# Cross-attention and FP4 feed-forward: gate and up in three chunks of 512, 512 and 384 columns in place of four of 352

## What is computed

```python
def fp4_linear(x, w):
    return einsum('bsk,nk->bsn', fp4_quant_dequant(x), fp4_quant_dequant(w))
def ffn(x, w_gate, w_up, w_down):          # w_gate, w_up: 1408 x 512, w_down: 512 x 1408
    gate, y = fp4_linear(x, w_gate), fp4_linear(x, w_up)
    h = silu(gate) * y
    return fp4_linear(h, w_down)
x = x + xattn(layernorm(x), ctx, ctx, mask, Wq, bq, Wk, bk, Wv, bv, Wo, bo)
x = x + ffn(layernorm(x), w_gate, w_up, w_down)
```

## Time and profile before

| | us |
|---|---|
| median of 3 executions (lowest, highest) | 2033.88 (2031.81, 2034.55) |
| the profiled execution | 2031.19 |
| its span, first to last instruction | 2029.3 |
| TensorE busy | 1898.9 (94%) |
| VectorE busy | 1770.0 (87%) |
| ScalarE busy | 1266.9 (62%) |
| GpSimd busy | 448.8 (22%) |

### The profile page before, as it was taken

How to read it: one execution, slowest core, us unless ns; L and a number is a source line. 1 busy time by engine, 2 the same in 40 slices (tenths; PEclk the granted TensorE clock), 3 DMA queues, 4 the chain that set the end, 5 groups by cost and what they waited for, 6 DMA issues and landing times.

```text
span 2029.3 us, 48669 instructions
## 1 busy us (share of the span) xinstructions
PE 1898.9 (94%) x17724; PEld 1192.0 (59%) x17792; DVE 1770.0 (87%) x2676; ACT 1266.9 (62%) x2613; POOL 448.8 (22%) x526
## 2 busy tenths in 40 slices
PE   6446899999999999999999999999999999999987
PEld 4334566656665666656665666666665666666643
DVE  7898889888899889888899889888899889888874
ACT  4575766676666666676666666676667666676421
POOL 5554221122112221122112211222112211222100
PEclk8667999999999999999999999999999999999998
DMA  5344566565766566566666566556765566556623
GB/s 170 105 114 95 109 144 144 127 132 132 156 133 132 130 145 139 129 133 134 149 138 132 130 147 138 127 134 136 154 131 132 130 149 137 126 134 133 128 56 84
DMA packets 716996, 265.34 MB, mean 131 GB/s; under 512 B 667930, under 2 KB 669878, under 8 KB 716958
## 3 DMA queue, kind: packets, MB, share of 16 engines
q1 hardware_dynamic: 715374, 264.85, 58.9%
q10 hardware_dynamic: 1584, 0.01, 0.1%
HBM read 66.34 MB, written 34.86 MB: 50 GB/s over the span
## 4 chain that ended last, share of the span: by engine, by line
PE 86%; DVE 6%; DMA 3%; issue 2%; POOL 1%; SPq 1%; ACT 1%; DVEq 0%; POOLq 0%; another core or an unknown queue 0%; ACTq 0%
PE psum L724 44%; PE psum L660 38%; PE psum L737 2%; PE psum L766 2%; DMA t_room<-halves 1%; DVE h_room L1278 1%; SPq L345 1%; PE psum L755 1%; POOL h_room L560 1%; DVE w_sc L1258 1%; POOL h_room L564 1%; DMA ph_room<-h_room 1%; DVE wguT L1246 1%; DVE h_room L1320 0%; DMA q_room<-in_L_xattn_Wk_dram 0%
## 5 line engine op out<-in xcount | busy, mean ns | idle before, releaser
L724 PE MATMUL psum<-wguT,t_room 128*128 128x352 bf16 x6144 | 943.1, 314 | 15.5 <-DVE h_room L1426 9.0
L724 PEld LDWEIGHTS psum<-wguT,t_room 128*128 128x128 bf16 x6144 | 597.4, 98 | 346.4 <-DVE h_room L1426 10.4
L660 PE MATMUL psum<-wdT,ph_room 128*128 128x512 bf16 x2108 | 469.8, 381 | 11.2 <-DMA ph_room<-h_room 10.9
L581 POOL TENSOR_TENSOR ln_var_eps<-ln_mean_var,eps 128x1 f32<-128x1 f32 x128 | 103.8, 811 | 1185.7 <-DVE ln_mean_var L1394 998.6
L660 PEld LDWEIGHTS psum<-wdT,ph_room 128*128 128x128 bf16 x2112 | 207.6, 98 | 263.3 <-issue 17.4
L982 ACT ACTIVATE silu_g<-psum 128x352 f32<-128x352 f32 x256 | 117.4, 459 | 380.2 <-PE psum L724 377.1
L988 ACT ACTIVATE probs<-psum,neg_max 128x77 f32<-128x77 f32 x1024 | 244.3, 350 | 3.7 <-DVE neg_max L1432 3.0
L1426 DVE TENSOR_TENSOR h_room<-silu_g,psum 128x352 f32<-128x352 f32 x256 | 132.2, 517 | 81.3 <-ACT silu_g L982 81.1
L1019 ACT ACTIVATE t_room<-psum,bq_col 128x128 bf16<-128x128 f32 x256 | 72.9, 367 | 185.7 <-PE psum L660 185.7
L660 PE MATMUL psum<-t_room,wqT 128*128 128x128 bf16 x3072 | 187.6, 222 | 0.8 <-DMA t_room<-halves 0.8
L660 PEld LDWEIGHTS psum<-t_room,wqT 128*128 128x128 bf16 x3072 | 177.7, 100 | 1.5 <-DMA t_room<-halves 1.1
(11 more groups left out here) (105 smaller groups left out, 2498.8 us busy)
## 6 DMA issues: line engine op xcount, KB each, us to landing
io_room<-in_x_dram SPq DMA_DIRECT2D x128, 256.0 KB, 2.8
x_scratch<-x_new SPq DMA_DIRECT2D x64, 256.0 KB, 2.0
x_cur<-x_scratch SPq DMA_DIRECT2D x64, 256.0 KB, 3.3
out_dram<-io_room SPq DMA_DIRECT2D x64, 256.0 KB, 2.4
t_room<-halves SPq DMA_TRANSPOSE x192, 3.2
raw<-in_L_ffn_w_down_dram SPq DMA_DIRECT2D x4, 704.0 KB, 4.3
raw<-in_L_ffn_w_gate_dram SPq DMA_DIRECT2D x11, 256.0 KB, 2.7
raw<-in_L_ffn_w_up_dram SPq DMA_DIRECT2D x11, 256.0 KB, 2.9
```

The costliest lines, as they stand in the source:

```text
L581: own.did(pool.tensor_tensor(var_eps, mean_var[:, 1:2], eps[:], ALU.add))
L660: ins = pe.matmul(dst, left(i), right(j), start=first and n == 0, stop=last and n == len(PRODUCTS) - 1)
L724: ins = pe.matmul(ps[:, 0:CW], left[:, i, kc, :], wguT[:, which, j, kc, cols], start=(kc == 0 and i == j), stop=(kc == KC - 1 and i == LO))
```

## The change

Gate and up are computed in chunks of 512, 512 and 384 columns. Chunk 0 goes to banks 0 and 1, chunk 1 to banks 2 and 3, chunk 2 to banks 0 and 1. `silu_g` becomes 512 wide (`CW`). In the step, chunk 1 of TensorE waits for `exp_done` alone, chunk 2 for chunk 0's `h_done`, the next weighted values for chunk 1's, the next chunk 0 for chunk 2's. On ScalarE the silu of chunk 1 is put behind `x_squares` and `h_high`; on VectorE `h_chunk(f, 1)` is put where `h_chunk(f, 2)` was. Head and tail are written for three chunks in the same way. In them the waits for chunk 0's `h_done` ahead of chunk 1 are gone, and where chunk 2 waited for `o_ready`, chunk 1 does now.

```diff
-    CHUNKS = 4
-    CW = INNER // CHUNKS
+    CHUNKS = 3
+    CW = 512
+    cut = [slice(c * CW, min((c + 1) * CW, INNER)) for c in range(CHUNKS)]
...
-        gate_ps = [bank[0], bank[0], bank[2], bank[0]]
-        up_ps = [bank[1], bank[1], bank[3], bank[1]]
+        gate_ps = [bank[0], bank[2], bank[0]]
+        up_ps = [bank[1], bank[3], bank[1]]
...
# TensorE
             def step(e, d, f, a, b, n, m):
                 if b is not None:
                     if d is not None:
-                        pe.wait_ge(h_done, d * CHUNKS + 3)
+                        pe.wait_ge(h_done, d * CHUNKS + 2)
                     weighted_values(b)
...
                 if f is not None:
-                    pe.wait_ge(h_done, f * CHUNKS + 1)
-                    gate_up_chunk(xqT, 1)
                     if n is not None:
                         pe.wait_ge(exp_done, 3 * n + 1)
+                    gate_up_chunk(xqT, 1)
+                    pe.wait_ge(h_done, f * CHUNKS + 1)
                     gate_up_chunk(xqT, 2)
-                    pe.wait_ge(h_done, f * CHUNKS + 2)
-                    gate_up_chunk(xqT, 3)
...
             projection(LAST - 1)
-            pe.wait_ge(h_done, 4 * TILES - 12)
+            pe.wait_ge(h_done, 3 * TILES - 9)
             pe.wait_ge(xqT_loaded, 16 * TILES - 32)
             gate_up_chunk(xqT, 0)
             weighted_values(LAST)
-            pe.wait_ge(h_done, 4 * TILES - 11)
+            pe.wait_ge(o_ready, TILES)
             gate_up_chunk(xqT, 1)
-            pe.wait_ge(o_ready, TILES)
+            pe.wait_ge(h_done, 3 * TILES - 8)
             gate_up_chunk(xqT, 2)
-            pe.wait_ge(h_done, 4 * TILES - 10)
-            gate_up_chunk(xqT, 3)
...
# ScalarE
-                if f is not None:
-                    silu_chunk(f, 1)
                 if a is not None:
                     x_squares(a)
                 if d is not None:
                     h_high(d)
                 if f is not None:
-                    silu_chunk(f, 2)
+                    silu_chunk(f, 1)
                 if a is not None:
                     xq_high(a)
                 if f is not None:
-                    silu_chunk(f, 3)
+                    silu_chunk(f, 2)
...
# VectorE
                 if n is not None:
                     probabilities_low(n, 1)
-                if f is not None:
-                    h_chunk(f, 1)
                 if a is not None:
                     first_round(xj)
...
                 if e is not None:
                     tile_out(e)
                 if f is not None:
-                    h_chunk(f, 2)
+                    h_chunk(f, 1)
                 if a is not None:
                     half_low(xq_h, xq, xq_hi, xq_lo, a)
                 if d is not None:
                     half_low(h_h, hq, h_hi, h_lo, d)
                 if f is not None:
-                    h_chunk(f, 3)
+                    h_chunk(f, 2)
```

More of the change, by code:

```diff
@@ L719, in gate_up_chunk @@
             def gate_up_chunk(left, c):
-                cols = slice(c * CW, (c + 1) * CW)
+                width = cut[c].stop - cut[c].start
                 for kc in range(KC):
@@ L723, in gate_up_chunk @@
                         for which, ps in ((0, gate_ps[c]), (1, up_ps[c])):
-                            ins = pe.matmul(ps[:, 0:CW], left[:, i, kc, :], wguT[:, which, j, kc, cols],
+                            ins = pe.matmul(ps[:, 0:width], left[:, i, kc, :], wguT[:, which, j, kc, cut[c]],
                                             start=(kc == 0 and i == j), stop=(kc == KC - 1 and i == LO))
@@ L865, in _ @@
             weighted_values(2)
+            pe.wait_ge(o_ready, 3)
+            gate_up_chunk(xqT, 1)
             pe.wait_ge(h_done, 1)
-            gate_up_chunk(xqT, 1)
-            pe.wait_ge(o_ready, 3)
             gate_up_chunk(xqT, 2)
-            pe.wait_ge(h_done, 2)
-            gate_up_chunk(xqT, 3)
             tiles(pe, step)
@@ L891, in _ @@
             projection(LAST)
-            pe.wait_ge(h_done, 4 * TILES - 8)
+            pe.wait_ge(h_done, 3 * TILES - 6)
             pe.wait_ge(xqT_loaded, 16 * TILES - 16)
             gate_up_chunk(xqT, 0)
-            pe.wait_ge(h_done, 4 * TILES - 7)
             gate_up_chunk(xqT, 1)
+            pe.wait_ge(h_done, 3 * TILES - 5)
             gate_up_chunk(xqT, 2)
-            pe.wait_ge(h_done, 4 * TILES - 6)
-            gate_up_chunk(xqT, 3)
             pe.wait_ge(out_ready, TILES - 4)
             down(LAST - 3)
-            pe.wait_ge(h_done, 4 * TILES - 4)
+            pe.wait_ge(h_done, 3 * TILES - 3)
             pe.wait_ge(xnT_loaded, 16 * TILES + 16)
             gate_up_chunk(xnT, 0)
-            pe.wait_ge(h_done, 4 * TILES - 3)
             gate_up_chunk(xnT, 1)
+            pe.wait_ge(h_done, 3 * TILES - 2)
             gate_up_chunk(xnT, 2)
-            pe.wait_ge(h_done, 4 * TILES - 2)
-            gate_up_chunk(xnT, 3)
             pe.wait_ge(out_ready, TILES - 3)
@@ L980, in silu_chunk @@
                 act.wait_ge(gu_ps, f * CHUNKS + (c + 1))
-                at_least(act, h_done, f * CHUNKS + (c - 1))
-                act.activation(silu_g[:, c % 2, :], gate_ps[c][:, 0:CW], ACT.Silu).then_inc(silu_done, 1)
+                at_least(act, h_done, f * CHUNKS + max(c - 1, 0))
+                width = cut[c].stop - cut[c].start
+                act.activation(silu_g[:, c % 2, 0:width], gate_ps[c][:, 0:width], ACT.Silu).then_inc(silu_done, 1)
             def exponentials(half, groups):
@@ L1201, in _ @@
             x_squares(1)
-            silu_chunk(0, 1)
             normed_high(4)
             o_high(2)
+            silu_chunk(0, 1)
+            xq_high(1)
             silu_chunk(0, 2)
-            xq_high(1)
-            silu_chunk(0, 3)
             tiles(act, step)
@@ L1219, in _ @@
             xq_high(LAST - 1)
-            silu_chunk(LAST - 2, 3)
+            silu_chunk(LAST - 2, 2)
             h_high(LAST - 3)
@@ L1228, in _ @@
             h_high(LAST - 2)
+            silu_chunk(LAST - 1, 1)
             silu_chunk(LAST - 1, 2)
-            silu_chunk(LAST - 1, 3)
             silu_chunk(LAST, 0)
+            h_squares(LAST - 1)
             silu_chunk(LAST, 1)
-            h_squares(LAST - 1)
             silu_chunk(LAST, 2)
-            silu_chunk(LAST, 3)
             h_high(LAST - 1)
@@ L1425, in h_chunk @@
                 dve.wait_ge(silu_done, f * CHUNKS + (c + 1))
-                own.did(dve.tensor_tensor(h[:, c * CW:(c + 1) * CW], silu_g[:, c % 2, :],
-                                          up_ps[c][:, 0:CW], ALU.mult), h_done, f * CHUNKS + (c + 1))
+                width = cut[c].stop - cut[c].start
+                own.did(dve.tensor_tensor(h[:, cut[c]], silu_g[:, c % 2, 0:width],
+                                          up_ps[c][:, 0:width], ALU.mult), h_done, f * CHUNKS + (c + 1))
             def maximum(n, half):
@@ L1645, in _ @@
             divide(x_job(1))
-            h_chunk(0, 1)
             first_round(x_job(1))
@@ L1650, in _ @@
             rescale(x_job(1))
+            h_chunk(0, 1)
+            half_low(xq_h, xq, xq_hi, xq_lo, 1)
             h_chunk(0, 2)
-            half_low(xq_h, xq, xq_hi, xq_lo, 1)
-            h_chunk(0, 3)
             half_low(o_h, o_sb, o_hi, o_lo, 2)
@@ L1670, in _ @@
             sums_inverse(LAST)
-            h_chunk(LAST - 2, 1)
             normalised(LAST)
@@ L1676, in _ @@
             divide(x_job(LAST - 1))
-            h_chunk(LAST - 2, 2)
+            h_chunk(LAST - 2, 1)
             half_low(o_h, o_sb, o_hi, o_lo, LAST)
@@ L1683, in _ @@
             rescale(h_job(LAST - 3))
-            h_chunk(LAST - 2, 3)
+            h_chunk(LAST - 2, 2)
             tile_out(LAST - 4)
@@ L1698, in _ @@
             divide(x_job(LAST))
-            h_chunk(LAST - 1, 1)
             first_round(x_job(LAST))
@@ L1706, in _ @@
             half_low(xq_h, xq, xq_hi, xq_lo, LAST)
+            h_chunk(LAST - 1, 1)
             h_chunk(LAST - 1, 2)
-            h_chunk(LAST - 1, 3)
             top(h_job(LAST - 1))
@@ L1714, in _ @@
             half_low(h_h, hq, h_hi, h_lo, LAST - 2)
-            h_chunk(LAST, 1)
             tile_out(LAST - 3)
@@ L1719, in _ @@
             rescale(h_job(LAST - 1))
+            h_chunk(LAST, 1)
             h_chunk(LAST, 2)
-            h_chunk(LAST, 3)
             top(h_job(LAST))
```

5 lines of the change are left out of this document (1 added, 4 removed).

## The result

The changed kernel takes 2058.37 us (median of 4, 2057.97 to 2058.94) against 2033.05 (2031.81 to 2034.55): a ratio of 1.0124, 95% interval 1.0107 to 1.0142, some 25 us slower. The forecast was 2055.

What follows compares the result with a forecast made beforehand. TensorE sets the time, with `pT` and `xnT` arriving just ahead of need. Terms 16.5 + 5.3 + 0.1 = 21.9 us on 2031.2 gave 2053.1, 2055.8 as a median; forecast 2055.0, range 2031 to 2073.

Steps and rivals of the forecast that it cites:

- Pace: TensorE's chunk matmuls: 2.5 ns each beside their columns, so 1536 fewer save 0.06 us a tile, 3.8 us in all.
- The closed loop from projection to queries: Each ordinary step: `xnT` lands too late, queries wait 0.36 us, period 28.81 us; 55 x 0.30 = 16.5 us.
- the rivals: Four alternatives: no stall 19%, wait on chunk 1's `h_done` or `xqT` 10%, falling clock 2%, costlier matmuls 1%.
- no wait of TensorE for `h_done`: Rival before weighted values: chunk 1's `h_done`, or `xqT` behind it, 0.5 us late; 2062 to 2083 us; 10%.
- the clock stayed at its upper level: Rival in the steady part: short stalls pull TensorE's clock down each period; 2130 us or more; 2%.
- What holds the second `pT`: SyncE's issue of the second `pT` transpose: released by VectorE's second `probabilities_low`, about 4.6 us before the weighted values.
- the VectorE chain: VectorE's unpaused stretch from `residual` after the projection to the second `probabilities_low`; predicted 0.17 us longer through `h_chunk(f, 0)`.
- The new-batch steps: Three steps at a new batch element: key loading delays the second `pT`; 1.77 us more each, 5.3 us together.
- the steady 0.30: Each ordinary period grows 0.30 us over the kernel before, through the stall before the queries.
- Head and tail: Before and after the steady loop: head 0 (bounds -2 and +2), tail +1.9, +0.8, -2.4; with 0.2 of pace, +0.1.

## Why the prediction was right, and where it was not

**Pace: right.** 28.45 us was computed as TensorE's own period, and it is what every three-chunk kernel shows in which nothing else waits.

**The closed loop from projection to queries: right in size.** Predicted were a wait of 0.36 us before the queries, the second `pT` 4.6 us before the weighted values and a period of 28.81. Measured: 0.35, 4.54 and 28.85. Three runs tie it to chunk 0's width (384 and 448 first: no loss; 512 first in the old kernel: the loss). Of the rivals, no wait of TensorE for `h_done` shows from 600 to 1800 us (chunk 1's product is done 15.1 us after the projection, 15.3 predicted, wanted after 16.20), and in the steady part the clock stayed at its upper level.

**What holds the second `pT`: half wrong.** The prediction said that the end of the VectorE chain releases it. It hangs on that and on SyncE's queue (first `pT`, mask), which end within 0.05 us of each other. Both start from VectorE's first `probabilities_low`. The late projection and the longer `h_chunk(f, 0)` stand ahead of that, so they make both late alike, and the sum did not feel the error. That was luck. An experiment built on this reading did feel it: with the low half of `xn` moved, 0 came instead of 21 us. The other one, with `h_chunk(f, 0)` moved, failed for a different reason (+25 us): it overlooked that the chain also waits for the second norm, and that GpSimd's part of it gets through beside `h_chunk(f, 0)`.

**The new-batch steps: too small.** Counted were 1.77 us for one period at each, 6.2 us for the six periods of the three with their share of the steady 0.30. The six grew by 8.9. The stalls were about as computed (1.99 + 0.42 us at the first, 2.6 by the count), but behind the first and the third TensorE's clock fell, and the next period was late too. The timeline of TensorE at the first of them, and the windows around the first and the second:

```profile
550.90 0.95 PE L738 MATMUL psum<-v_cur,ph_room 117*128 117x33 bf16 x32 [1.99 <-DMA ph_room<-p_h]
552.27 4.48 PE L661 MATMUL psum<-t_room,wqT 128*128 128x128 bf16 x48 [0.42 <-DMA t_room<-halves]
```

```profile
1016.00:1027.00 11.00, 9.72 (x156) 6.53 (x159) 6.70 (x13) 5.17 (x9) 1.47 (x4) 1.00 0.92 194
549.00:560.00 11.00, 8.52 (x98) 6.71 (x100) 6.59 (x14) 3.54 (x8) 1.00 (x3) 0.84 0.99 212
```

The 48 query matmuls took 4.48 us instead of 2.85, at 0.84 granted over the window; at the second new batch element, behind stalls of 2.06 + 0.30 us, the clock stayed (the first of the two rows), and why it did stays open. The term had no clock in it.

**Head and tail: right in the sum, in part by luck.** The weighted values of the fifth tile start at 229.98 in both kernels, so the head gave 0.0. But in the changed kernel a stall of 4.96 us for `pT` stands right before them, which the prediction didn't have; it eats what went elsewhere. Nor is the head the same each time: the two kernels with 384 columns first and the later mask, whose head is the same code, reach the sixth tile's weighted values at 258.77 and at 263.51 in their traces. From the next-to-last weighted values on, the tail took 0.04 us less (37.47 + 104.15 against 35.56 + 106.10), where +0.1 was predicted. The stall at `o_ready` grew from 3.62 to 6.49 (6.2 predicted), and the two of 1.18 went. Two pieces that the prediction didn't count cancel: the last period is 1.9 us longer (1.6 of it is chunk 0), and `o_ready` comes 7.45 us after the last weighted values start instead of 8.72.

**Sum in the trace.** The spans differ by 27.05 us: 18.2 in 52 ordinary periods (predicted 15.6), 8.9 at the new batch elements (6.2), 0 in head and tail (0.1). Of the 2.6 us more in the ordinary periods, 0.6 fall on the first behind the head (30.69 against 29.75), in which the 48 query matmuls took 4.47 us as above. The medians differ by 25.3 us and not by 27: the traced execution of the kernel before lies 1.9 us below its median. So the trace exceeds the 21.9 us of the prediction by 5.2 us, while the forecast of 2055 missed the median by 3.4; part of that closeness is the baseline, which had been taken 0.8 us too high from three executions.

## What to carry to other kernels

In a pipelined loop, an operation between two points of a closed chain costs what it grows beyond the chain's slack, in every period, even when the engine's total work is unchanged or less: put the narrow piece inside the chain and the wide ones outside. Before moving work, list all that a late transfer waits for; where two conditions end together, moving one alone gains nothing and can cost. A wait in the tail is a place for work that is ready, such as a down projection of an older tile.

## What the runs showed of the hardware

- GpSimd's 128x1 operations took 0.19 to 0.55 us where they started beside a VectorE operation that reads a bank or has one input in SBUF, or while VectorE was idle. Where they met operations with two SBUF inputs they took 1.3 to 1.9 us and ended 0.05 to 0.4 us behind the end of one. By the Trainium skill (SBUF — State Buffer, SBUF: two separate sides) the two engines share a pair of ports under an exclusive lock for a whole instruction, which a VectorE operation with two SBUF inputs also takes. The trace agrees in that none of the slow ones ended before such an operation had; one of them, though, in the run with `h_chunk(f, 0)` later, outlasted the end of the rescaling and ended only with `probabilities_low`, which had started after it.
- TensorE's clock fell behind stalls of 1.99 + 0.42 us (0.84 granted from 549 to 560 us). It stayed at the upper level at the next new batch element, where the stalls were as long (2.06 + 0.30 us, 1.00 granted), and behind 0.29 + 0.25.
- Issuing the 9.6 KB mask held SyncE for 0.64 to 1.15 us between the two `pT` transposes in the changed kernel's ordinary steps, and for 0.35 to 0.51 us behind `oT`.
